# First attention of a gated cross-attention stack: reciprocals and divisions by halves of heads, with a semaphore count for each part

## The reference, cut to what matters

```python
q = (query @ wq.T + bq); k = (key @ wk.T + bk); v = (value @ wv.T + bv)   # then split in heads
scores = jnp.einsum('bhqd,bhkd->bhqk', q, k) * scale
scores = jnp.clip(scores, -100.0, 100.0)
scores = jnp.where(mask == 0, -jnp.inf, scores)
attn = jax.nn.softmax(scores, axis=-1)
out = jnp.einsum('bhqk,bhkd->bhqd', attn, v)
return out @ wo.T + bo
...
x = x + jnp.tanh(g_xattn[0]) * _L0_xattn_ref(_layernorm(x, axis=-1), ctx_1024, ctx_1024, mask, ...)
```

## Time and profile before

| | us |
|---|---|
| median of 3 runs | 2836.78 |
| lowest, highest | 2831.11, 2843.86 |
| the profiled execution, its own time | 2842.46 |
| its span on the core | 2840.7 |
| PE busy (share of the span) | 2697.2 (95%) |
| DVE busy | 1632.8 (57%) |
| ACT busy | 1484.6 (52%) |
| POOL busy | 1042.2 (37%) |
| the 64 clips of the first attention start at | 33.0 to 448.0 |

### The profile page before, as it was taken

The page is one execution under the profiler, slowest core; times in us unless marked ns, Lnnn a source line. Parts: engine busy times, 40 slices in busy tenths (PEclk is TensorE's granted clock), DMA queues, the critical chain, the costliest instruction groups (busy, mean ns, idle before and its releaser), DMA issues. The chain is left out here.

```text
span 2840.7 us, 47238 instructions
## 1 busy us (share of the span) xinstructions
PE 2697.2 (95%) x18014; PEld 1530.0 (54%) x18014; DVE 1632.8 (57%) x2693; ACT 1484.6 (52%) x3650; POOL 1042.2 (37%) x823
## 2 busy tenths in 40 slices
PE   6999988999999999999999989999999999999999
PEld 4555544444444467777777655566444444444444
DVE  7888885755555456655665478887633423333232
ACT  4888885333223256666666479999433222332221
POOL 2445452375455646666666401111102201220111
PEclk9999999999999999999999989999999999999999
DMA  4011104211111279999999710101400000000000
GB/s 156 21 55 50 50 16 146 67 46 49 49 49 35 75 253 293 273 289 287 283 288 293 177 60 31 61 31 50 144 34 1 30 30 30 1 30 30 15 1 30
DMA packets 152320, 277.75 MB, mean 98 GB/s; under 512 B 20000, under 2 KB 28960, under 8 KB 152096
## 3 DMA queue, kind: packets, MB, share of 16 engines
q1 hardware_dynamic: 115232, 207.39, 20.7%
q0 software_dynamic: 36864, 67.34, 11.2%
HBM read 198.86 MB, written 75.89 MB: 97 GB/s over the span
## 5 line engine op out<-in xcount | busy, mean ns | idle before, releaser
L1424 POOL DMA_INDIRECT ids<-sh_tk,sh_su x256 | 269.8, 1054 | 245.6 <-PE sh_gu L55 87.9
L55 PE MATMUL ex_gu<-ex_xT,ex_h 128*128 128x256 f16 x3072 | 347.3, 273 | 1.7 <-ACT ex_xT L1697 1.7
L55 PEld LDWEIGHTS ex_gu<-ex_xT,ex_h 128*128 128x128 f16 x3072 | 301.1, 98 | 51.0 <-ACT ex_xT L1697 1.9
L1829 POOL DMA_INDIRECT xp<-ex_oo,ex_to x128 | 241.8, 1889 | 177.5 <-ACT ex_oo L1731 136.3
L2408 POOL TENSOR_TENSOR fe_prodT<-fe_pp,fe_prodT 128x512 f16<-128x512 f32 x64 | 76.8, 1199 | 604.4 <-ACT fe_prodT L2175 604.4
L533 PE MATMUL at_g<-id,at_p 128*128 128x128 f32 x1280 | 211.8, 290 | 43.7 <-POOL at_p L928 23.7
L1555 DVE SCALAR_TENSOR_TENSOR ex_h<-ring,ex_h 128x1024 f16<-128x1024 f32 x128 | 151.1, 1222 | 151.6 <-ACT ex_h L1545 151.6
L533 PEld LDWEIGHTS at_g<-id,at_p 128*128 128x128 f32 x1280 | 165.6, 170 | 114.3 <-issue 46.7
L701 ACT ACTIVATE at_s<-at_s,at_mx 128x154 f32<-128x154 f32 x512 | 210.3, 416 | 0.0
L927 POOL TENSOR_TENSOR at_p<-at_s,at_rs 128x1024 f32<-128x1024 f32 x64 | 121.5, 1899 | 234.2 <-DVE at_rs L826 234.2
L2319 DVE SCALAR_TENSOR_TENSOR ring<-fe_g,fe_nf,ring 128x512 f32<-128x512 f32 x32 | 24.0, 751 | 293.1 <-PE fe_g L2079 293.1
(11 more groups left out here) (355 smaller groups left out, 5679.9 us busy)
## 6 DMA issues: line engine op xcount, KB each, us to landing
ring<-L_ffn_expert_gate_up_w SPq DMA_DIRECT2D x64, 1024.0 KB, 7.9
ring<-L_ffn_expert_down_w SPq DMA_DIRECT2D x64, 512.0 KB, 8.9
ring<-x SPq DMA_DIRECT2D x24, 1024.0 KB, 5.8
x<-ring SPq DMA_DIRECT2D x16, 1024.0 KB, 5.1
zrows<-hm_zs SPq DMA_DIRECT2D x32, 256.0 KB, 2.0
xp<-ring SPq DMA_DIRECT2D x8, 1024.0 KB, 5.1
out<-ring SPq DMA_DIRECT2D x8, 1024.0 KB, 4.2
ring<-xp SPq DMA_DIRECT2D x7, 1024.0 KB, 5.6
```

Of the source, the lines that this page charges most:

```text
L55: mm = nc.tensor.matmul(out, lhs(a, k), rhs(b, k), start=start and i == 0 and j == 0, stop=stop and i == n - 1 and j == 2)
L1424: e.indirect_dma_start(ids, bass.IndirectOffsetOnAxis(slotu[b % 2][:, t, j:j + 1], 0), pair[b % 2][:, t, j, :], None, bounds_check=SLOTS - ...
L1829: e.indirect_dma_start(dst, bass.IndirectOffsetOnAxis(to[:, n:n + 1], 0), o32[y % 2][:, t, :], None, bounds_check=T + SLOTS - 1, oob_is_er ...
```

## The change

Only the first attention changes. The 8 reciprocals of a unit are made in two instructions of 4 (`summed(j, part)`). The one for heads 0 to 3 is written ahead of the clip of the same step, behind the waits that the clip has, and waits for the first half of the exponentials alone; the one for heads 4 to 7 stays behind the clip. `rsum` counts 2 a unit. GpSimd's multiply for 128 columns becomes one for each half, each waiting for its own reciprocals and each counted; the remainder stays one instruction. `prob` counts 3 a unit, and TensorE waits for the count of its own part ahead of each of the three batches of transposes.

```diff
--- before.py
+++ after.py
@@ -619,17 +619,18 @@
                     mm.then_inc(s["s_mm"], 1)
                 i = n - behind
                 if 0 <= i < UNITS:
-                    e.wait_ge(*((s["prob"], i + 1) if L0 else (s["expd"], 2 * i + 1)))
+                    e.wait_ge(*((s["prob"], 3 * i + 1) if L0 else (s["expd"], 2 * i + 1)))
                     keys_turned(i, 0, 0)
                 for what in plan[n][:1]:
                     piece(*what)
                 if 0 <= i < UNITS:
-                    if not L0:
-                        e.wait_ge(s["expd"], 2 * i + 2)
+                    e.wait_ge(*((s["prob"], 3 * i + 2) if L0 else (s["expd"], 2 * i + 2)))
                     keys_turned(i, 4, 1)
                 for what in plan[n][1:]:
                     piece(*what)
                 if 0 <= i < UNITS:
+                    if L0:
+                        e.wait_ge(s["prob"], 3 * i + 3)
                     keys_turned(i, HH, 2)
             if maps_ahead:
                 e.wait_ge(s["expd"], 2 * UNITS - 1)
@@ -692,7 +693,7 @@
                 if not L0 and i >= NP:
                     e.wait_ge(s["p_mm"], 3 * (i - NP) + 3)
                 if i >= 3:
-                    e.wait_ge(s["rsum"], i - 2)
+                    e.wait_ge(s["rsum"], 2 * (i - 2) if L0 else i - 2)
                 if not L0 and i == 0 and part == 0:
                     e.wait_ge(s["blank"], NP)
                 for h in range(HG):
@@ -815,15 +816,16 @@
                                            inv[B % 3][:, k, :, None].broadcast_to([P, 2 * HH, HD]), ALU.mult, ALU.mult
                                            ).then_inc(s["f_out"], 1)
 
-            def summed(j):
+            def summed(j, part=1):
 
                 if not 0 <= j < UNITS:
                     return
-                e.wait_ge(s["expd"], 2 * j + 2)
+                e.wait_ge(s["expd"], 2 * j + part + 1)
                 if L0:
                     if j >= 3:
-                        e.wait_ge(s["prob"], j - 2)
-                    e.reciprocal(rs[j % 3][:, :], sm[j % 3][:, :]).then_inc(s["rsum"], 1)
+                        e.wait_ge(s["prob"], 3 * (j - 2))
+                    half = slice(HG * part, HG * part + HG)
+                    e.reciprocal(rs[j % 3][:, half], sm[j % 3][:, half]).then_inc(s["rsum"], 1)
                 else:
                     to = inv[j // UPB % 3][:, j % TPB, j // TPB % 2 * HH:j // TPB % 2 * HH + HH]
                     e.reciprocal(to.rearrange("p (g j) -> p j g", j=HG), sm[j % 3][:, :].rearrange("p (j g) -> p j g", j=HG)
@@ -856,9 +858,10 @@
                     if i >= 3:
                         e.wait_ge(s["expd"], 2 * (i - 2))
                     if L0 and i >= NS:
-                        e.wait_ge(s["prob"], i - NS + 1)
+                        e.wait_ge(s["prob"], 3 * (i - NS + 1))
                     halves = [slice(HG * part, HG * part + HG) for part in range(2)]
                     if L0:
+                        summed(n - lag - 1, 0)
                         e.scalar_tensor_tensor(sc[i % NS][:, :, :], S[:, :, 0:CTX], -100.0,
                                                lim[B % 2][:, t:t + 1, :].broadcast_to([P, HH, CTX]),
                                                ALU.max, ALU.min).then_inc(s["clip"], 1)
@@ -919,18 +924,21 @@
                     pb, sb_, rb = prob[i % 2], sc[i % NS], rs[i % 3]
                     if i >= 2:
                         e.wait_ge(s["p_mm"], 3 * (i - 2) + 3)
-                    e.wait_ge(s["rsum"], i + 1)
                     main = pb[:, 0:HH * P].rearrange("p (h n) -> p h n", h=HH)
                     rem = pb[:, HH * P:].rearrange("p (j r n) -> p r j n", r=HG, n=HD)
                     srem = sb_[:, :, P:CTX].rearrange("p (r j) n -> p r j n", r=HG)
                     rrem = rb[:, :].rearrange("p (r j) -> p r j", r=HG)[:, :, :, None]
-                    e.tensor_tensor(main, sb_[:, :, 0:P], rb[:, :, None].broadcast_to([P, HH, P]), ALU.mult)
+                    for part in range(2):
+                        h = slice(HG * part, HG * part + HG)
+                        e.wait_ge(s["rsum"], 2 * i + part + 1)
+                        e.tensor_tensor(main[:, h, :], sb_[:, h, 0:P], rb[:, h, None].broadcast_to([P, HG, P]), ALU.mult
+                                        ).then_inc(s["prob"], 1)
                     e.tensor_tensor(rem[:, :, :, 0:REM], srem, rrem.broadcast_to([P, HG, HH // HG, REM]), ALU.mult
                                     ).then_inc(s["prob"], 1)
                 for what in plan[n]:
                     piece(*what)
             if L0:
-                e.wait_ge(s["prob"], UNITS)
+                e.wait_ge(s["prob"], 3 * UNITS)
             e.wait_ge(s["x_bias" if L0 else "x_out"], TPB * NB)
 
         def sync():
```

## The result

| | before | after |
|---|---|---|
| median, same chip, 6 runs each (us) | 2835.36 | 2844.83 |
| lowest, highest | 2830.68, 2843.86 | 2839.70, 2850.85 |
| the profiled execution | 2842.46 | 2843.57 |
| first attention: first matmul of the stage behind it | 483.17 | 493.49 |

The ratio after to before is 1.0034 [1.002, 1.0048]: within the 0.5% named in the prediction, yet a small loss of about 9.5 us that the interval sets apart from zero. The two profiled executions differ by 1.1 us only, but the first attention itself ends 10.3 us later. What differs the other way is late: from 941 us on, the profiled execution of after took 1901 us, and that of before from 931 us on 1910 us, in stages that the change doesn't touch. So the first attention is read by its own end.

The account below looks back on a forecast made before the run. Regular blocks were taken as bound by a VectorE run, then a TensorE run. Blocks +1.9, start +1, clock +1.6, last block −2.5 and tail −1.2 gave +0.8 us: about 2837.5 us, no change, 8 in 10 for 2823 to 2850.

Parts of the forecast that it names:

- No gain in a regular block: Regular blocks: TensorE's waits for GpSimd vanish, but the values piece still waits for VectorE's copy; gain 0, not 2.7 us.
- my 1.04: GpSimd's division: a half multiply was estimated to take 1.04 us.
- VectorE's run +0.22 us: Regular blocks: two added reciprocals lengthen VectorE's run before the copy by 0.22 us, bounds 0.2 and 0.6.
- The collisions: Regular blocks: VectorE and GpSimd block each other at other instructions; net 0, bounds −0.8 and +1.0 us a block.
- Two more waits a unit on TensorE: Ahead of the second and third transpose batches: 0.1 us a block, bounds 0 and 1 us a block.
- Clock +1.6 us, bounds −3.3 and +6.5: Regular blocks: one more block with TensorE's clock dropped to 1.2 GHz; bounds no drops left and all six blocks.
- Last block and tail −3.7 us: End of the first attention: a shorter loop of clip and division, −2.5 us, and a shorter serial last unit, −1.2.
- My tail term of −1.2: Serial last unit: earlier transposes bring the end 1.2 us forward, bounds −0.3 and −1.6.
- Start +1: First two blocks: added reciprocals find little cover on VectorE; +1 us, at most 1.8.
- Rival A: First attention: TensorE's waits for GpSimd are on the path after all; −23.8 us, 2813 us, chance 0.13.
- Rival B: Regular blocks: VectorE's run passes 14.3 us, clock drops in all six, end gives nothing; +17.9, 2854.7 us, chance 0.09.
- My own sign: Regular blocks: the forecast is right if a block still takes 51.7 to 52.3 us.

Follow-up runs that it names:

- fill_after: The changed kernel with the first batch of transposes issued five times in the step of TensorE's long wait before the late values piece; 0.9998 of before.
- lim_before: The kernel before with three mask pieces moved from the steps of VectorE's 13 us run to steps 5 and 6 of the block before; 0.9952 of before.
- bias_after: The changed kernel with GpSimd's bias adds moved four steps later, out of the steps of VectorE's run; 0.9964 of before.
- hoist_one: The kernel before with its one 8-column reciprocal written ahead of the clip in place of behind it, no instruction added; 1.0018 of before.
- onewait: The changed kernel, but TensorE waits once a unit, ahead of the first transposes, for all three parts of the division; 1.0026 of before.

## Why the prediction was right, and which term failed

The median (2844.83) lies in the range of 2823 to 2850 and within 0.5% of before, as forecast, but not by the sum as I had it: 7 us above my 2837.5, with the clock term far too low and the terms of VectorE's run and of the end too high. That it lies inside is in part luck. With the clock as measured and every other term as forecast the sum is +13.6 us, 2850 us, the edge of the range. (The low bounds of the terms add up to −14.1, which makes 2823 and not 2824.)

- **No gain in a regular block: held.** TensorE no longer waits for GpSimd, and waits for the copy instead. From L797 to L584 it was 223.16 − 210.08 = 13.08 us, before 13.09 (217.20 − 204.11). `fill_after` and `lim_before` show the same by other ways. The half multiply took 1.042 us for my 1.04.
- **VectorE's run +0.22 us: it came to 0.** From L797 to the end of the copy: 12.83 us, before 12.84. The reciprocals cost what I said, 0.09 to 0.12 us start to start. The collisions paid for them: L768 −0.43, L771 −0.45, L774 +0.74, together −0.14 where I took 0; the rest is small shares of other instructions. The row was the right free price, and L774 did wait out L909 as forecast, in every block. In `bias_after`, without GpSimd beside it, L774 fell from 1.43 to 0.48 us. The Trainium skill (SBUF — State Buffer, "SBUF: two separate sides") has a shared port pair that VectorE in a 2-port mode or GpSimd holds as an exclusive lock for a whole instruction. The traces agree: L774, started 0.41 us behind the bias add, ended 0.33 us behind its end; which mode it ran in no trace shows.
- **Two more waits a unit on TensorE: 0.1 us a block at most**, as I took. `fill_after` has all of them, and its six blocks average 51.75 us, against 51.67 for a block of before without a drop.
- **Clock +1.6 us, bounds −3.3 and +6.5: this step failed.** The cause was the one named, as far as `fill_after` shows it: work in the lightly used stretch ahead of L584 took the drops away. But both factors were too small. I took one more block with a drop, and it was all six. I took 1.63 us a drop from the earlier trace rows, and it was 2.95 us, since the half clock lasted 6.8 us instead of 3.4. Six by 2.95 less two by 1.63 is +14.4 us; the six blocks lost 14.5. My upper bound took the higher count with the lower price. Nothing in the rows of before showed a drop of the longer kind in a regular block, but the earlier trace rows showed TensorE at 1.2 GHz for 10 us where it waited more. The stretch of 3.4 us was no ceiling.
- **Last block and tail −3.7 us, within bounds of −6.0: it was −5.9.** From the start of the last block to L797 2.2 us were won (442.38 − 423.19 = 19.19, before 428.42 − 407.02 = 21.40). VectorE waited 2.75 us for ScalarE there for the 3.67 of the earlier trace rows. The other 3.6 us lie behind it. Up to L797 TensorE's clock helped: its mean was 0.91 over this stretch, before 0.76. At the end TensorE's two waits for GpSimd were 0.66 and 0.34 us instead of 2.10, and the values piece ran in 1.06 instead of 1.93 us (the rows at 475.68 and, before, 463.16). My tail term of −1.2 had no clock in it, and its bound of −1.6 was too narrow. But the shorter waits don't make the clock stay up each time. `fill_after` has the same 0.66 and 0.34 us, its values piece took 1.93 us, and its last block and tail 72.1 us.
- **Start +1: it was +1.7.**

The sum is +1.7 + 14.5 − 5.9 = +10.3 us where I had +0.8, and the medians moved by 9.5. Rival A is refuted: no regular block got shorter. Rival B said that the clock would fall in all six blocks and that L774 would wait out L909; both came true, and with them its sign, L774 over 1.4 us and blocks over 53 us. My own sign, blocks of 51.7 to 52.3 us, did not. It failed in that VectorE's run didn't grow, its own point of decision (14.3 us), and in giving the last block nothing. I had tied two independent things into one rival, "every term must go badly"; the clock needed none of the others.

**What stays open.** (1) What exactly makes the clock fall. It fell in two of six blocks of before (waits 1.17, 1.34, 0.34), in two of `hoist_one` (0.56, 0.33, 1.8), in five of `bias_after` (1.96 at the end) and of `onewait` (0.75, 0.80, 1.30), and in all of after (0.69, 2.16). Neither the longest wait nor their sum orders these. (2) Why the stage behind the first attention (from its first to its last matmul on `sh_LG`) takes 447.2 us in some executions and up to 458.5 in others, of before and of after alike (447.3 and 453.1; 447.2 and 456.2). It goes with the chip: where before's median was 2835 or 2840 us, all four profiles show 447.2 or 447.3, where it was 2860 or 2863, all eight show 452.9 to 458.5. That is 6 to 11 us of (3): why one kernel takes 2835 us on one chip and 2863 on another. (4) Why an end earlier by 4.5 us in `fill_after` doesn't show in its ratio (0.9998), and one earlier by 2.3 us in `hoist_one` stands beside a ratio over 1. A profile is one execution, and the drops differ between executions.

## What to carry to other kernels

A wait that an engine shows is worth nothing before it is known what comes last: here three moved VectorE instructions won 0.5%, and dividing earlier, which TensorE visibly waited for, won nothing in a regular block. Where idle time can't be removed, look at what its new place does to TensorE's granted clock, and price that with the worst drop in the trace, in every repetition of the block, as a rival of its own. If a block repeats and TensorE waits once in it, cheap work of its own put into the wait can be worth more than shortening someone else's instruction; here it gave back what the change had cost, and no more (0.9998 of before).

## What the runs showed of the hardware

- The same 2.85 us of idle time in a block cost nothing or 1.6 us a block in the kernel before and 2.95 us in the changed one. Sixteen transposes of repeated work in the wait (20 took 2.40 us) gave all of it back in the blocks, 51.8 for 54.6 us.
- After a stretch with waits TensorE ran at 1.2 GHz for 3.4 or 6.8 us: L584 took 1.93 for 1.06 us and L586 2.08 for 1.12.
- A VectorE operation on f32 that takes 0.48 us alone took 1.43 when it was issued beside GpSimd's bias add, and the add, 1.27 us alone, took 1.51, as it started while another VectorE operation of that kind (L771) still ran. In `hoist_one` the operation in front fell beside the add, took 1.35 us and its neighbour 0.48.
- A reciprocal of 4 columns shows 0.17 us and costs 0.09 to 0.12 in a row of VectorE instructions.
- Removing TensorE's waits of 1.17 and 1.34 us for the division was worth nothing in a regular block: the 2.51 us came back at the next waits, 0.69 for the clip and 1.82 more for the copy.
